# Expert weights as the stationary operand, streamed per tile, in a decoder-block kernel on one core

## The reference

```python
probs = softmax(xf @ router_w.T)               # 4096 tokens, 8 experts
topv, topi = top_k(probs, 2)                   # two experts for each token, renormalised
g = einsum('nd,edf->nef', xf, gate_w) + gate_b # 256 -> 512
u = einsum('nd,edf->nef', xf, up_w) + up_b
h = silu(g) * u
expert_out = einsum('nef,efd->ned', h, down_w) + down_b
y = einsum('ne,ned->nd', probs, expert_out)
x = layernorm(x + y)
```

## Time and profile before

| | |
|---|---|
| median of 3 runs | 1710.3 us |
| the profiled execution | 1718.2 us, its span 1716.4 us |
| PE busy | 1523.2 us (89%) |
| DVE, ACT, POOL busy | 1087.5, 724.6, 677.0 us |
| DMA | 177 MB, mean 103 GB/s |

### The profile page before, as it was taken

How to read it: one execution, slowest core, us unless ns; L and a number is a source line. 1 busy time by engine, 2 the same in 40 slices (tenths; PEclk the granted TensorE clock), 3 DMA queues, 4 the chain that set the end, 5 groups by cost and what they waited for, 6 DMA issues and landing times. The chain is left out here.

```text
span 1716.4 us, 30448 instructions
## 1 busy us (share of the span) xinstructions
PE 1523.2 (89%) x10698; PEld 1079.5 (63%) x10698; DVE 1087.5 (63%) x2352; ACT 724.6 (42%) x1572; POOL 677.0 (39%) x530
## 2 busy tenths in 40 slices
PE   6999954899999999957999999997798999999980
PEld 3555523788888887633677777776555666666650
DVE  4899866577777874531557777888555444454443
ACT  4877751234434444543455455552242222222224
POOL 1354447222333311010344566654545544444440
PEclk9999975699999999988999999998899999999995
DMA  3233446645555535053034124110733322323326
GB/s 105 87 144 114 160 149 185 181 107 163 151 161 137 155 72 186 35 200 120 15 99 138 31 74 145 50 37 13 255 56 38 47 47 44 50 44 46 49 35 202
DMA packets 186939, 177.15 MB, mean 103 GB/s; under 512 B 79639, under 2 KB 147787, under 8 KB 186667
## 3 DMA queue, kind: packets, MB, share of 16 engines
q1 hardware_dynamic: 163963, 145.23, 28.1%
q0 software_dynamic: 17216, 22.95, 8.1%
q10 hardware_dynamic: 5616, 7.08, 1.2%
HBM read 111.19 MB, written 64.01 MB: 102 GB/s over the span
## 5 line engine op out<-in xcount | busy, mean ns | idle before, releaser
L2476 POOL DMA_INDIRECT y<-vw,idx x71 | 125.5, 1768 | 190.7 <-DVE vw L2622 180.3
L622 DVE SCALAR_TENSOR_TENSOR conv_y<-conv_in,taps,conv_y 128x512 f32<-128x512 f32 x192 | 161.4, 850 | 24.2 <-ACT conv_y L470 19.5
L1867 PE MATMUL xQ<-late,last 128*128 128x512 f32 x256 | 128.5, 625 | 8.9 <-ACT late L2029 4.8
L2540 PE MATMUL xO<-late,aT 128*128 x568 | 135.4, 381 | 0.8 <-DVE vw L2620 0.8
L2519 PE MATMUL xS<-w_gu,kT 128*128 x288 | 132.2, 602 | 0.8 <-ACT kT L2566 0.6
L375 PE MATMUL ps_j<-xnT,w_qkv 128*128 128x512 f32 x256 | 122.4, 602 | 0.0
L1815 POOL TENSOR_TENSOR sc<-sc,den 128x1232 f32<-128x1232 f32 x32 | 72.0, 2250 | 113.6 <-DVE den L2286 113.5
L2607 DVE TENSOR_TENSOR sc<-xS,last 128x512 f32<-128x512 f32 x107 | 73.7, 692 | 60.6 <-PE xS L2519 57.2
L2540 PEld LDWEIGHTS xO<-late,aT 128*128 128x128 f32 x568 | 103.1, 192 | 12.5 <-issue 1.2
L2620 DVE TENSOR_TENSOR vw<-xO,late 128x256 f32<-128x256 f32 x71 | 30.1, 424 | 121.4 <-PE xO L2540 121.4
L996 POOL DMA_DIRECT2D x<-x1t x32 | 18.2, 568 | 223.5 <-ACT x1t L1348 218.4
(11 more groups left out here) (354 smaller groups left out, 3675.1 us busy)
## 6 DMA issues: line engine op xcount, KB each, us to landing
carried<-qkvg SPq DMA_DIRECT2D x64, 256.0 KB, 4.0
qkvg<-tok SPq DMA_DIRECT2D x4, 2048.0 KB, 6.7
qkvg<-gate SPq DMA_DIRECT2D x8, 1024.0 KB, 9.5
qks<-qkvg SPq DMA_DIRECT2D x32, 256.0 KB, 4.6
steps<-step SPq DMA_DIRECT2D x30, 256.0 KB, 4.4
qkvg<-carried SPq DMA_DIRECT2D x3, 2048.0 KB, 6.5
vw<-even SPq DMA_DIRECT2D x4, 1232.0 KB
xin<-in_x SPq DMA_DIRECT2D x9, 512.0 KB, 10.0
```

The lines of the kernel that those rows point to most:

```text
L622: y = nc.vector.scalar_tensor_tensor(conv_y[m % 4][:], conv_in[b][:, m, k:k + BT], taps[:, m, k:k + 1], conv_y[m % 4][:], ALU.mult, ALU.add)
L1867: mm = pe.matmul(Q[:], w_q[:, c, j * P:(j + 1) * P], x1T[:, c, :], start=c == 0, stop=c == KD - 1)
L2476: nc.gpsimd.indirect_dma_start(out=s["y"].rearrange("t p d -> (t p) d"), out_offset=bass.IndirectOffsetOnAxis(ap=x.idx[j % 8][:, 0:1], axi ...
L2540: mm = pe.matmul(x.pD[:, 0:D], x.hT[q][:, k, :], w_d[:, bass.ds(e, 1), k, :], start=k == 0, stop=k == FK - 1)
```

## The change

It does these things together:

- The gate and up weights are no longer kept for all experts. A ring of RING = 4 buffers of 1 MB takes the weights of the tiles j, j+1, j+2 and j+3; SP loads them tile by tile (`weights(j)`), once the gate and up products of tile j-4 are done (`gu_done`). 71 tiles load 1 MB each; the 8 MB at blocks 1 to 4 are gone.
- The weights are the stationary operand, 128x128 pieces, and the turned tokens (128 columns) the moving one: 4 pieces f by 2 over c, for gate and for up. The products come out as hidden x tokens, which is the form that `down` needs as its stationary operand. `h_turned` and ACT's copy (`h_out`) fall away, and DVE writes the hidden rows straight into `hT`.
- The biases are now one value for each partition. They are loaded at block 1 with 8 transfers of 4-byte elements (`load_biases`) and read with a step of 0 over the tokens; the 4 MB spread to all partitions are gone.
- `down` follows one tile behind instead of two, and so does `out`. SP loads the list entries 3 tiles ahead of the weights in its own order. `between(7)`, the last x2 store, stands behind `rows(10)` and `weights(7)`.

```diff
-                if 1 <= n <= 4:
-                    load_experts_early(sp, a, s, (2 * n - 2, 2 * n - 1))
+                if n == 1:
+                    load_biases(sp, a, s)
                 if n == BLOCKS - 1:
                     sp.wait_ge(ss_done, BLOCKS)
                     load_experts_late(sp, a, s)
-                    sp.wait_ge(sc_done, 3 * TILE_N)
-                    load_experts_last(sp, a, s)
...
+def load_biases(eng, a, s):
     for k, n in enumerate(("L0_ffn_gate_b", "L0_ffn_up_b")):
+        for c in range(FK):
+            eng.dma_start(s["b_gu"][:, k, c, :], a[n].rearrange("e (k p) -> p k e", p=P)[:, c, :],
+                          allow_slow_non_contiguous=True).then_inc(s["last_in"], 16)
...
 def expert_sync(nc, sp, a, x, s, between):
...
+    def rows(j):
         q = j % 8
         if j == HEAD:
             sp.wait_ge(x.listed, 4)
             sp.wait_ge(x.list_out, 16 * BLOCKS * BLK * 2)
         if j >= 8:
             sp.wait_ge(x.o_done, j - 7)
...
+    def weights(j):
+        if j >= RING:
+            sp.wait_ge(x.gu_done, 2 * (j - RING) + 2)
+        e = expert(sp, s, j)
+        for k, n in enumerate(("L0_ffn_gate_w", "L0_ffn_up_w")):
+            sp.dma_start(s["w_gu"][j % RING][:, :, k * FF:(k + 1) * FF],
+                         a[n][bass.ds(e, 1)].rearrange("n (k p) f -> p (n k) f", p=P)).then_inc(x.w_in[j % RING], 16)
+
+    for j in range(LIST_LEAD):
+        rows(j)
+    for j in range(FT):
+        if j + LIST_LEAD < FT:
+            rows(j + LIST_LEAD)
+        weights(j)
         between(j)
...
+    def gate_up(j):
         pe.wait_ge(x.xT_sb, j + 1)
+        pe.wait_ge(x.w_in[j % RING], 32 * (j // RING) + 32)
...
         for k, to in enumerate((x.pG[q], x.pU[q])):
-            for c in range(KD):
-                mm = pe.matmul(to[:], x.xsT[q][:, c, :], w_gu[:, bass.ds(e, 1), c, k * FF:(k + 1) * FF],
-                               start=c == 0, stop=c == KD - 1)
+            for f in range(FK):
+                for c in range(KD):
+                    mm = pe.matmul(to[:, f * P:(f + 1) * P], w_gu[j % RING][:, c, k * FF + f * P:k * FF + (f + 1) * P],
+                                   x.xsT[q][:, c, :], start=c == 0, stop=c == KD - 1)
             mm.then_inc(x.gu_done, 1)
...
         if j < FT:
             known[j] = expert(pe, s, j)
-            gate_up(j, known[j])
+            gate_up(j)
         if j + 1 < FT:
             x_turned(j + 1)
-        if 1 <= j <= FT:
-            h_turned(j - 1)
-        if j >= 2:
-            down(j - 2, known.pop(j - 2))
+        if j:
+            down(j - 1, known.pop(j - 1))
         between(j)
...
-            nc.vector.tensor_tensor(to, frm[:], b_gu[:, bass.ds(e, 1), k * FF:(k + 1) * FF], ALU.add).then_inc(done, 1)
+            nc.vector.tensor_tensor(to.rearrange("p (k j) -> p k j", j=P), frm[:].rearrange("p (k j) -> p k j", j=P),
+                                    b_gu[:, k, :, bass.ds(e, 1)].broadcast_to([P, FK, P]), ALU.add).then_inc(done, 1)
...
-        nc.vector.tensor_tensor(x.g[q], x.g[q], x.u[q], ALU.mult).then_inc(x.h_done, 1)
+        nc.vector.tensor_tensor(x.hT[q].rearrange("p k j -> p (k j)"), x.g[q], x.u[q], ALU.mult).then_inc(x.h_done, 1)
...
         if j < FT:
             known[j] = expert(dve, s, j)
             biased(j, known[j])
-        if j >= 2:
-            out(j - 2, known.pop(j - 2))
-        if j < FT:
             hidden(j)
+        if j:
+            out(j - 1, known.pop(j - 1))
```

More of the change, by code:

```diff
@@ L1772, in between @@
                     store_x2(BLOCKS - 1)
-            expert_sync(nc, sp, x, s, between)
+            expert_sync(nc, sp, a, x, s, between)
             sp.wait_ge(x2_out, 32 * BLOCKS)
@@ L2379, in _ @@
             expert_vector(nc, dve, x, s, last_residual, between)
[L2384 to L2392, removed]
+LATE_LOADS, LAST_LOADS, RING = NE + 1, 2 * FK, 4
 def load_experts_late(eng, a, s):
@@ L2417, in __init__ @@
         self.x2_out, self.list_out, self.listed, self.at_done = x2_out, list_out, listed, at_done
+        self.w_in = [sem(f"e_w_in{q}") for q in range(RING)]
         self.rows_in = [sem(f"e_rows_in{q}") for q in range(8)]
@@ L2431, in expert, with expert_sync @@
     return eng.value_load(s["tile_e"][0:1, j:j + 1], min_val=0, max_val=NE - 1)
-def expert_sync(nc, sp, x, s, between):
+def expert_sync(nc, sp, a, x, s, between):
     lists = s["list"].rearrange("(n p) c -> n p c", p=P)
@@ L2438, in expert_sync @@
     sp.wait_ge(x.list_out, 16 * HEAD_BLOCKS * BLK * 2)
-    for j in range(FT):
+    def rows(j):
         q = j % 8
@@ L2499, in expert_tensor @@
     w_gu, w_d = s["w_gu"], s["w_d"]
-    pe.wait_ge(s["early_in"], EARLY_LOADS * 16)
     pe.wait_ge(x.listed, 2)
@@ L2509, in x_turned @@
         mm.then_inc(x.xT_done, 1)
-    def gate_up(j, e):
+    def gate_up(j):
         q = j % 2
         pe.wait_ge(x.xT_sb, j + 1)
+        pe.wait_ge(x.w_in[j % RING], 32 * (j // RING) + 32)
         if j >= 2:
@@ L2535, in down @@
             pe.wait_ge(s["late_in"], LATE_LOADS * 16)
-        pe.wait_ge(x.hT_sb, j + 1)
+        pe.wait_ge(x.h_done, j + 1)
         if j:
@@ L2544, in expert_tensor @@
     known = {}
-    for j in range(FT + 2):
+    for j in range(FT + 1):
         if j == HEAD:
@@ L2571, in silu @@
         nc.scalar.activation(x.g[j % 2], x.g[j % 2], ACT.Silu).then_inc(x.silu_done, 1)
-    def h_out(j):
-        act.wait_ge(x.hT_done, j + 1)
-        if j >= 2:
-            act.wait_ge(x.d_done, j - 1)
-        nc.scalar.activation(x.hT[j % 2], x.pH[:].rearrange("p (k j) -> p k j", k=FK), ACT.Copy).then_inc(x.hT_sb, 1)
     x_out(0)
-    for j in range(FT + 1):
+    for j in range(FT):
         if j + 1 < FT:
             x_out(j + 1)
-        if j:
-            h_out(j - 1)
-        if j < FT:
-            silu(j)
+        silu(j)
         between(j)
@@ L2603, in biased @@
         if j >= 2:
-            dve.wait_ge(x.hT_done, j - 1)
+            dve.wait_ge(x.h_done, j - 1)
         for k, (to, frm, done) in enumerate(((x.g[q], x.pG[q], x.gb_done), (x.u[q], x.pU[q], x.ub_done))):
             dve.wait_ge(x.gu_done, 2 * j + k + 1)
-            nc.vector.tensor_tensor(to, frm[:], b_gu[:, bass.ds(e, 1), k * FF:(k + 1) * FF], ALU.add).then_inc(done, 1)
+            nc.vector.tensor_tensor(to.rearrange("p (k j) -> p k j", j=P), frm[:].rearrange("p (k j) -> p k j", j=P),
+                                    b_gu[:, k, :, bass.ds(e, 1)].broadcast_to([P, FK, P]), ALU.add).then_inc(done, 1)
     def hidden(j):
         q = j % 2
+        if j >= 2:
+            dve.wait_ge(x.d_done, j - 1)
         dve.wait_ge(x.silu_done, j + 1)
         dve.wait_ge(x.ub_done, j + 1)
-        nc.vector.tensor_tensor(x.g[q], x.g[q], x.u[q], ALU.mult).then_inc(x.h_done, 1)
+        nc.vector.tensor_tensor(x.hT[q].rearrange("p k j -> p (k j)"), x.g[q], x.u[q], ALU.mult).then_inc(x.h_done, 1)
     def out(j, e):
@@ L2750, in build @@
             ex = lambda n, shape, dt=F32: experts.enter_context(nc.sbuf_tensor(n, shape, dt))
-            s["w_gu"] = ex("w_gu", [P, NE, KD, 2 * FF])
+            s["w_gu"] = [ex(f"w_gu{q}", [P, KD, 2 * FF]) for q in range(RING)]
+            s["b_gu"] = ex("b_gu", [P, 2, FK, NE])
             s["late"] = ex("late", [P, NE * FK * D + NE * D])
@@ L2755, in build @@
             s["last"] = ex("last", [P, XW // P * BT + KD * XW + (XH * CTX + P - 1) // P * D])
-            s["b_gu"] = s["last"][:, 0:NE * 2 * FF].rearrange("p (e f) -> p e f", e=NE)
-            s["early_in"], s["late_in"], s["last_in"] = sem("early_in"), sem("late_in"), sem("last_in")
+            s["late_in"], s["last_in"] = sem("late_in"), sem("last_in")
             cross_stage(nc, a, s)
```

5 lines of the change are left out of this document (removed).

## The result

The changed kernel takes 1738.2 us (median of 4 runs, 1715.6 to 1741.6), the kernel before 1710.4 (4 runs, 1709.4 to 1716.6). The prediction was 1703 us in a range of 1688 to 1734. The kernel is slower by more than its measurement can hide, and the time lies above the range.

The account below looks back on a forecast made before the run. PE alone was taken to set the pace. 65 tiles at -0.33 (-21.5), +2.6 for eight without gain, store +13, clock +2.5, end -4 gave -7.4 us: 1710.3 to 1703 us, range 1688 to 1734.

Parts of the forecast that it names:

- The end: From gate_up(70) to the last scatter: 12.7 us instead of 16.7, so -4 us.
- PE's tile: Expert tiles on PE: h_turned's 0.44 us goes, gate and up add 0.11; 5.82 becomes 5.49 us, 0.33 gained per tile.
- rival 3: Weight loads of gate and up not covered by products: tile 6.0 us, 1736 us in all; 6% chance.
- Tiles paced by POOL: Eight tiles with list scatters alongside: scatters 5.9 us apart whatever PE does, so no gain there, +2.6 us.
- 1 MB for each tile hidden: Expert weight loads take 2.8 us of each 5.49 us tile, total DMA share 0.84, hidden: no cost.
- rival 4: Expert weights come late because DMA saturates above 0.84: tile 6 us or more, about 1735 us; 4% chance.
- The same traffic beside the scatters: Weight loads beside the y scatters: scatters can slide past them, costed at nothing, with +1.6 us per scatter as other end.
- rival 1: The chain of y scatters binds: landing 5.6 us, tile 6.0 us, 1733 us in all; 20% chance.
- The late store: Last x2 store goes out near 1268.5, delaying scatter(0) and pausing PE ahead of x_turned(5): +13 us, lower clock +2.5.
- Rival 2: The late x2 store costs little, by quicker order at tile 3 or PE not missing gather(5): 1687 us; 12% chance.

Follow-up runs that it names:

- run 1: Changed kernel with only the first four tiles' gate and up weights loaded, later tiles using what lies in the ring: 1695.0 us.
- run 2: Changed kernel with odd tiles added to a second buffer, each scatter waiting only for the one before the last: 1703.0 us.
- run 4: Changed kernel with SP issuing weights(j) before rows(j+3), so weights no longer wait for `o_done`: 1704.1 us.
- run 12: Changed kernel with one added PE wait, ahead of gate_up(17), until scatter(14) has landed: 1722.8 us, median of 10.
- run 8: Changed kernel, order untouched, with the up weights not loaded from tile 4 on: 1699.5 us.
- run 3: Changed kernel with the last x2 store issued behind weights(3) instead of weights(7): 1724.5, 1721.6, 1701.9 and 1688.5 us.
- runs 4 and 5: The second is the changed kernel with both weights(j) before rows(j+3) and the last x2 store behind weights(3): 1697.1 us.
- Run 6: Changed kernel with weights before rows and early x2 store, but weights the moving operand, `h_turned` back and down two tiles behind: 1741.4 us.
- run 9: Run 6 with rows led by two tiles instead of three: 1721.2 us.
- run 10: Changed kernel with weights before rows, the x2 store behind weights(3), and rows led by two tiles instead of three: 1691.6 us.
- run 1 to 11: The second is the changed kernel with expert weights loaded only for the first four tiles and the last x2 store early: 1685.6 us.

## Why the prediction was wrong, step by step

The stretch from gather(0) to the last scatter, cut at the starts of gate_up(5) and gate_up(70), holds the sum. Before it took 440.0 us (36.5, 386.7 and 16.7). Differences to that, in us:

| | to gate_up(5) | 5 to 70 | to the last scatter | in all |
|---|---|---|---|---|
| forecast | +15.5 | -18.9 | -4 | -7.4 |
| changed kernel | +15.6 | +12.5 | -1.5 | +26.5 |
| run 1, without the loads | +11.0 | -24.6 | -5.3 | -19.0 |

Of the error of 34 us, 31 sit between gate_up(5) and gate_up(70), and 28 of those from gate_up(16) to gate_up(66), in the steady tiles (302.0 us, against 290.9 before and 274.4 at 0.33 less for each tile). The end gave 1.5 us instead of 4. Outside the stretch the two profiles differ by 3.2 us, by which gather(0) comes earlier in the changed kernel (1232.34 and 1235.58).

**PE's tile: right.** Passes at 0.112 us, a tile of 5.52 us; the 0.111 of the earlier trace rows was the right one of the two, and the loads of 32 pieces are covered (rival 3 is out). Run 1 has the gain in full, 5.7 us more than forecast: its steady tiles gain 0.30 us each.

**Tiles paced by POOL: near in the number, wrong in the reason.** I had no gain in them "whatever PE does". In the changed kernel gate_up(5) to gate_up(16) takes 72.7 us against 72.6 before. But without the loads, in run 1, it takes 64.1, 8.5 less than before in 11 tiles, so it was the loads that held them up.

**1 MB for each tile hidden: right.** In run 2 the share is 0.83 at PE's full pace (forecast 0.84), and nothing waits for w_gu in the changed kernel (rival 4 is out).

**The same traffic beside the scatters: this step failed.** It said: "But the scatter's place is free to slide. [...] After 3 us of sliding, the scatter moves its data when the 2.8 us burst is over. So I cost it at nothing". The mechanism was named and then priced at zero. What the runs showed in its place is +11.1 us over the kernel before in the 50 steady tiles, where the loads alone cost 26, and all of it goes when only the wait from scatter to scatter (run 2) or the common release (run 4) goes. Two things were wrong in the step.

- The place at a lag of about 3 us exists (run 12; run 8 with half of the loads, at 1.6 to 3.2). But nothing makes the chain stop there on its way. It enters the steady tiles far behind: while list scatters share POOL, scatters are up to 9.4 us apart, and the lag is 10.8 at tile 11. From there it goes to about 8.5 and stays.
- At 8.5 the slack is gone. The step had "over 7 us to slide in", and that count was right: of the 13.5 us from `o_done` of tile s to x_turned(s+5) in run 1, 1.9 go to the scatter ahead of the gather, and the gather lands after 2.8 us at the least and after 4.1 in run 3, which has the same loads. That leaves 7.5 to 8.8 us. At a lag of 8.5 x_turned(s+5), three tiles on, just misses its gather (at 1499.64 in the steady stretch PE had waited 0.6 us for one). The price of overlap was also too low, 2.4 us and more where I took 1.6.

Why the chain stays at 8.5 is argued. One reading is a second place of rest, one tile of 5.5 us behind the first, beside the next tile's burst. The other is that the chain just runs into the end of the slack, where `o_done` and the weights slip along with it. Both give the same number here, and no run separates them.

That is rival 1, which had 20%: it gave a tile of 6.0 us (measured 6.03) and 1733 us (measured 1738). Which lag an execution takes is my explanation of the spread of 26 us here and of 36 in run 3, where the kernel before has 7 in its four runs and 14 in twelve others; only profiled executions show a lag, so for the others it is argued.

**The cure follows from the release.** When the weights are released by `gu_done` (runs 4 and 5), they go out 3.3 us after `o_done` instead of 1.9, and the chain rests at a lag of 3.7 to 5.8 us, inside the slack. A place one tile behind that would lie beyond the slack, so the chain has nowhere else to rest; this last is argued. Run 6 against run 9 shows the same by the opposite sign, with nothing but the lead of the rows changed. A lead of two in the turned form (run 10) is less steady: its lag goes up to 7.0.

**The late store: right.** +15.6 us to gate_up(5) in the changed kernel, forecast 13 + 2.5, with the scatter at 1272.7 (1276, counted on a start that came 3.2 us later), the pause of 14.01 us and the lower clock. Down took 1.7 us more by the clock, and the first half of gate_up(5) 0.8. What an early store then saves is less, 7 us from run 4 to 5 and 7.5 to 9.4 from run 1 to 11: POOL sets the pace behind it and gives part back. Rival 2 is out.

**A rule on the price.** Beside the measured 2.4 us and more: the Trainium skill ("DMA: Bandwidth & Descriptors", Latency and other measured facts) puts the access latency of HBM at 0.2 us on average and at 2 us under high load, and calls the confirmation of the write most of a transfer's fixed cost. The measured increase agrees in size with that. No run here separates the confirmation from the queueing of packets.

**What stays open:** what knocks the chain from one lag to the other in a given execution, and why the stretch from gate_up(5) to gate_up(16), with its list scatters, is 7.4 us longer with the loads than without them even when they are released apart (run 4 against run 1).

## What to carry to other kernels

When added traffic is to share the machine with a serial chain of transfers, ask first which event releases each. If one event releases both, they can meet in every iteration, and an average share with room to spare (0.84 here) doesn't rule that out. Slack absorbs such a meeting only if it is larger than the lag with which the chain enters the loop, so work out that lag too (10.8 us here, for 7.5 to 8.8 of slack).

A kernel whose four runs spread by 26 us where the old one's spread by 7 may have two regimes. Look at the lag of the chain in each profile before believing a median.

## What the runs showed of the hardware

An accumulating scatter of 128 rows of 256 floats, waited for before the next, repeats every 4.4 us alone and every 6.8 to 7.1 us in the mean when a 1 MB load is issued with it or within 1 us behind it. With two such chains taking turns, the same loads cost the pace nothing (5.52 us a scatter, at a DMA share of 0.83): at this pace the load lengthens the landing and doesn't limit how many scatters get through.

After a pause of 14 us of PE, its products ran at the lower clock (0.57 granted in the mean over the first 6 us, against 1.00), as after the pause ahead of tile 0:

```profile
1281.00:1287.00 6.00, 6.00 (x26) 5.28 (x25) 2.01 (x7) 2.42 (x4) 4.78 (x5) 0.57 0.36 47
```
